# Four-layer graph network on one core: the loads and gathers of layer one's first four chunks wait for an earlier point of the set-up

## What the kernel computes

```python
src = node_irreps[edge_index[0]]
feats = {0: src[:, :M][:, :, None], 1: src[:, M:].reshape(E, M, 3)}
sh = {0: sh0, 1: sh1, 2: sh2}
for idx, (le, ln, lo) in enumerate(COMBOS):
    base = jnp.einsum('ijk,ei,emj->emk', CG[le, ln, lo], sh[le], feats[ln])
    msg[lo] = msg[lo] + jnp.einsum('io,eik->eok', W[idx], base)
agg0 = jax.ops.segment_sum(msg[0].reshape(E, M), tgt, num_segments=N)
agg1 = jax.ops.segment_sum(msg[1].reshape(E, 3 * M), tgt, num_segments=N)
...
x = _layernorm(x + _L0_gnn_ref(x, edge_index, edge_weight1, edge_attr_3, edge_attr_5, L0_gnn_W), axis=-1)
x = _layernorm(x + _L1_gnn_ref(x, edge_attr_2, L1_gnn_weight, edge_index), axis=-1)
x = _layernorm(x + _L2_gnn_ref(...), axis=-1)
x = _layernorm(x + _L3_gnn_ref(...), axis=-1)
```

## Time and profile before

| | us |
|---|---|
| median of 3 runs | 17409.68 (17409.63 to 17410.06) |
| the profiled execution | 17404.72 |
| its span | 17402.7 |
| busy: POOL | 12932.6 (74%) |
| busy: DVE | 12117.7 (70%) |
| busy: PE | 6419.3 (37%) |
| busy: ACT | 3285.1 (19%) |

### The profile page before, as it was taken

How to read it: one execution, slowest core, us unless ns; L and a number is a source line. 1 busy time by engine, 2 the same in 40 slices (tenths; PEclk the granted TensorE clock), 3 DMA queues, 4 the chain that set the end, 5 groups by cost and what they waited for, 6 DMA issues and landing times. The chain is left out here.

```text
span 17402.7 us, 138752 instructions
## 1 busy us (share of the span) xinstructions
PE 6419.3 (37%) x33487; PEld 5142.6 (30%) x33487; DVE 12117.7 (70%) x15588; ACT 3285.1 (19%) x5336; POOL 12932.6 (74%) x13715
## 2 busy tenths in 40 slices
PE   1000000000444454545330000000006999999995
PEld 0000000000333333333320000000005878878774
DVE  5666666674899999999663232223326999999996
ACT  0000000000222222222541101111102223222321
POOL 6777777777677777777757777777777777777776
PEclk9555555555777777777665555555558999999998
DMA  4333333331111111111332222222222222222221
GB/s 103 97 96 97 97 98 97 98 97 47 28 28 28 28 28 28 28 28 25 130 130 59 59 57 59 58 59 58 59 53 45 55 55 53 56 53 56 53 56 36
DMA packets 744244, 1076.69 MB, mean 62 GB/s; under 512 B 375703, under 2 KB 508493, under 8 KB 731294
## 3 DMA queue, kind: packets, MB, share of 16 engines
q0 software_dynamic: 417376, 477.82, 12.5%
q1 hardware_dynamic: 250851, 398.14, 8.2%
q10 hardware_dynamic: 75736, 197.70, 3.1%
HBM read 684.92 MB, written 389.48 MB: 62 GB/s over the span
## 5 line engine op out<-in xcount | busy, mean ns | idle before, releaser
L1937 POOL DMA_INDIRECT s_arena<-d_t,s_arena x3125 | 3086.5, 988 | 971.3 <-issue 943.6
L1898 POOL DMA_INDIRECT d_pay<-s_arena x3125 | 3026.9, 969 | 997.7 <-issue 931.0
L1977 POOL DMA_INDIRECT s_arena<-d_t,s_arena x3125 | 2960.6, 947 | 1032.6 <-issue 952.0
L1955 POOL DMA_INDIRECT s_arena<-d_t,s_arena x3125 | 2948.5, 944 | 981.7 <-issue 952.1
L1649 PE MATMUL psall<-s_arena 128*128 128x500 bf16 x1875 | 835.4, 500 | 4365.4 <-DVE psall L881 3637.1
L992 DVE TENSOR_TENSOR s_arena<-s_arena,psall 128x2400 f32<-128x2400 f32 x125 | 332.0, 2656 | 2712.1 <-DMA s_arena<-d_t,s_arena 2712.1
L1649 PEld LDWEIGHTS psall<-s_arena 128*128 128x128 bf16 x1875 | 222.5, 119 | 4783.3 <-DVE psall L881 3708.7
L1756 PE MATMUL psall<-s_w2r,s_arena 128*128 128x384 f32 x4250 | 1514.0, 491 | 5.9 <-DVE s_arena L1090 5.2
L1838 PE MATMUL psall<-s_tails,s_mfix 128*128 128x32 f32 x6 | 1.9, 412 | 3972.8 <-DVE s_tails L1198 3972.8
L1756 PEld LDWEIGHTS psall<-s_w2r,s_arena 128*128 128x128 f32 x4250 | 1271.0, 317 | 64.3 <-DVE s_arena L1090 6.1
L1099 DVE TENSOR_REDUCE s_arena<-s_arena 128x64 f32<-128x1024 f32 x875 | 1248.1, 1438 | 0.0
(11 more groups left out here) (304 smaller groups left out, 17923.9 us busy)
## 6 DMA issues: line engine op xcount, KB each, us to landing
s_arena<-d_t,s_arena POOLq DMA_INDIRECT x9375, 2.5
d_scan<-s_arena ACTq DMA_DIRECT2D x313, 400.0 KB, 2.6
s_arena<-d_ew SPq DMA_DIRECT2D x126, 800.0 KB
s_arena<-d_pay SPq DMA_DIRECT2D x33, 1650.0 KB, 6.8
d_inj<-s_agg SPq DMA_DIRECT2D x125, 400.0 KB, 3.9
s_arena<-d_inj SPq DMA_DIRECT2D x125, 400.0 KB, 3.4
d_pay<-s_arena POOLq DMA_INDIRECT x3125, 2.2
d_fold<-s_arena ACTq DMA_DIRECT2D x33, 1250.0 KB, 4.9
```

Source lines behind the costliest of these rows:

```text
L1898: e.indirect_dma_start(pay_d, bass.IndirectOffsetOnAxis(ap=S1.adr[s4][:, t:t + 1], axis=0), S1.pay[s4][:, 33 * t:33 * t + 33], None).then_ ...
L1937: e.indirect_dma_start(L3.gb[s][:, t], None, T3_d, bass.IndirectOffsetOnAxis(ap=L3.idx[s][:, t:t + 1], axis=0)).then_inc(sem(f"g3_{s}"), 16)
L1955: e.indirect_dma_start(L0.gb[s][:, t * 128:(t + 1) * 128], None, T0_d, bass.IndirectOffsetOnAxis(ap=L0.idx[s][:, t:t + 1], axis=0)).then_i ...
L1977: e.indirect_dma_start(L2.gb[k][:, t * 96:(t + 1) * 96], None, T2_d, bass.IndirectOffsetOnAxis(ap=L2.idx[k][:, t:t + 1], axis=0)).then_inc ...
```

## The change

`room0(c)` takes the place of `v0(c - 4, "g")` in the two waits of layer one. For chunks 0 to 3 it is `mk["split"]`, from chunk 4 on what it was. So that the four chunks have numbers known in Python, chunks 0 to 4 are written out on SP and POOL, and the loop has 30 rounds. The same transfers are started in the same order, and the other three engines' code is the same.

```diff
--- before.py
+++ after.py
@@ -838,6 +838,10 @@
         def v0(c, name):
 
             return c * PER0 + (mk["base0"] + AT0[name])
+
+        def room0(c):
+
+            return mk["split"] if isinstance(c, int) and c < 4 else v0(c - 4, "g")
 
         def vector_scan0(e, c, s2):
 
@@ -1947,9 +1951,9 @@
 
         def gpsimd_chunk0(e, c, i, k):
             s = k % 4
-            e.wait_ge(sem(f"ix_{s}"), nth4(0 if i is None else i, k) * 16)
+            e.wait_ge(sem(f"ix_{s}"), nth4(i, k) * 16)
             held(e)
-            e.wait_ge(dv.h, v0(c - 4, "g"))
+            e.wait_ge(dv.h, room0(c))
             held(e)
             for t in range(T):
                 e.indirect_dma_start(
@@ -1959,11 +1963,11 @@
         def gpsimd_edges0(e):
             for s in range(4):
                 e.wait_ge(sem(f"t0_st{s}"), 16 * (7 if s == 0 else 6))
-            assert v0(-4, "g") >= mk["split"]
-            gpsimd_chunk0(e, 0, None, 0)
-            with e.Fori(0, 31) as i:
+            for c in range(5):
+                gpsimd_chunk0(e, c, 0, c)
+            with e.Fori(0, 30) as i:
                 for k in range(1, 5):
-                    gpsimd_chunk0(e, i * 4 + k, i, k)
+                    gpsimd_chunk0(e, i * 4 + (k + 4), i + 1, k)
 
         def gpsimd_edges2(e):
             barrier(e, "gpsimd")
@@ -2126,12 +2130,12 @@
 
         def sync_chunk0(e, c, i, k):
             s = k % 4
-            e.wait_ge(dv.h, v0(c - 4, "g"))
+            e.wait_ge(dv.h, room0(c))
             e.sem_inc(idle2, 1)
             e.dma_start(L0.idx[s].bitcast(I32), src_v[:, bass.ds(c * T, T)]).then_inc(sem(f"ix_{s}"), 16)
             for o, w_, a_ in ((0, 1, ew1), (1, 3, ea3), (4, 5, ea5)):
                 e.dma_start(L0.at[s][:, o * T:(o + w_) * T], a_.rearrange("(p t) d -> p (t d)", p=P)[:, bass.ds(c * (T * w_), T * w_)]).then_inc(sem(f"at0_{s}"), 16)
-            if i is None:
+            if k == 0:
                 lo_, n = 0, 14
             else:
                 lo_, n = i * (106 * 33) + (14 + 27 * (k - 1) - (k == 4)) * 33, 26 + (k < 3)
@@ -2139,10 +2143,11 @@
             e.dma_start(inj_d[0:E, :].rearrange("(p t) f -> p (t f)", p=P)[:, bass.ds(c * 800, 800)], agg[:, 924:1724]).then_inc(sem("fill_z"), 16)
 
         def sync_edges0(e):
-            sync_chunk0(e, 0, None, 0)
-            with e.Fori(0, 31) as i:
+            for c in range(5):
+                sync_chunk0(e, c, 0, c)
+            with e.Fori(0, 30) as i:
                 for k in range(1, 5):
-                    sync_chunk0(e, i * 4 + k, i, k)
+                    sync_chunk0(e, i * 4 + (k + 4), i + 1, k)
             e.wait_ge(sem("fill_p"), 125 * 16)
             e.wait_ge(sem("fill_z"), 125 * 16)
```

## The result

| | median us | runs | lowest to highest |
|---|---|---|---|
| kernel before | 17410.3 | 22 | 17408.1 to 17416.7, and one of 29563.9 |
| changed kernel | 17381.4 | 22 | 17377.1 to 17391.8 |

The ratio is 0.9983, with a 95% interval of 0.9977 to 0.9990, which is 17 to 40 us; the single run of 29563.9 is left out of it. The medians differ by 28.9 us. The sum in the prediction was 28.3, and it had 0.94 on a change within 0.2%. That the two lie 0.6 us apart is closer than this interval can show.

What follows compares the result with a forecast made beforehand. POOL's unbroken row of gather starts was taken to bound layer one; 29.3 - 0.5 - 0.5 = 28.3 us off the median 17409.7 gives 17381.4, range 17375 to 17393.

Steps and rivals of the forecast that it cites:

- The bound: Layer one is one unbroken row of POOL gather starts, 1.2483 us apart; starting it earlier gains as much, 29.31 us.
- Late issue and crowded engines: POOL's 29.6 us idle before layer one: SP issues its load late, at 182.39, and it lands slowly beside edge_weight, 18.4 us.
- First cost: SP's 3.6 MB for four chunks now run beside the set-up's last 12 block gathers: 0 to 4.0 us, 0.5 taken.
- Second cost: First gathers now run beside VectorE's last set-up steps, which may hold their starts: 0 to 8.2 us, 0.5 taken.
- Third cost: First gathers of layer one land late beside ACT's edge_weight, but 57 us of cover before chunk 4 make it 0.
- Rival 1: In layer one POOL's queue holds only 9 gathers beside edge_weight, losing 10 us: 17391, at the extreme 17423; chance 0.08.
- Rival 2: Chunk 0's source numbers still come late, or another POOL wait ends last; nothing gained, 17409.7; chance 0.03.
- Rival 3: Layer one's starts lose their even pace as VectorE's steps hold some: 137 us added, 17519; chance 0.03.
- The marks: Times the changed kernel's profile should show, from SP's first load at about 156.5 to POOL's last gather at about 4073.

Runs made afterwards that it cites:

- POOL's old wait: Changed kernel with the old wait put back on POOL's gathers alone, SP's loads still early; 17422.9 us against 17440.3 of the kernel before, ratio 0.9989.
- pieces in the kernel before: Kernel before with ACT's edge_weight issued in 125 pieces, one with each chunk, instead of one transfer; 17426.4 us against 17440.3, ratio 0.9991.
- The four-fold `edge_weight`: Changed kernel with three more transfers like edge_weight's, into a tensor nobody reads; 17460.5 us, ratio 1.0011 against the kernel before.

## Why the prediction was right, point by point

- **The bound.** An unbroken row of POOL starts, and a gain of what its first start moves. Right on the chips where POOL is the bound: the first gather moved 29.3, 17.6 and 15.4 us (changed, POOL's old wait, pieces in the kernel before; the first against the split) and the time 28.9, 17.4 and 13.9. The four-fold `edge_weight` gave the same sum with the other sign: -28.9 + 46.6 = +17.7, measured +20.2. The first of these times is from 22 runs of each kernel; the others rest on medians whose intervals are wider than the differences between them. On the slow chips the premise does not hold (VectorE does not wait for the gathers there), and the intervals are too wide to say whether the number does.
- **Late issue and crowded engines.** Both shown, at 12.9 us for the first (what is left when the engines are free, the load's own 2.7 us in it) and 16.7 for the rest. What the prediction didn't say is that POOL's own wait stood right behind SP's load, at 184, and would have kept 12 us of the 29. It took the edit on POOL as done and did not price it.
- **First cost, SP's transfers (0 to 4.0, 0.5 taken).** Measured 0: 14.85 us in three executions, with nothing, 2.8 and 4.2 MB of SP's beside the block gathers, within the cover of 7.5 us each time. In the changed kernel these landed in 3.7 us (median), where I expected 6 to 7 from the table's stores: that row was too dear, and the bound of 4.0, which came from a stretch beside `edge_weight`, does not apply to SP's transfers alone.
- **Second cost, VectorE's set-up (0 to 8.2, 0.5 taken).** Measured 0: the 40 short steps, 8.36 us in all from 176.2 to 190.1, now run beside gathers, and none of these starts takes over 0.95 us. So the bound of 8.2 us, in which every one of these steps of 0.1 to 0.8 us held POOL in full, has no case here. A long step of the split does hold a start (3.23 us instead of 0.94 beside the 3.41 us of line 404). Length alone does not decide it: beside the 8.22 us of line 905, in layer one of the same execution, no start takes over 1.007. What decides it stays open.
- **Third cost, edge_weight (0).** The result was right, but three terms on the way to it were not. The share of POOL's queue was put at 16 packets per us, and a gather at 36 packets, so 0.45 gathers. From 185 to 215 us it is 639 packets, or 21 per us. They carried 1.31 MB, 2 KB each, so a gather is 32 packets (the 0.09 MB of the earlier trace rows was too coarse for this), and 21 per us are 0.67 gathers:

```profile
q10 hardware_dynamic: 9510, 0.95, 88.3%
q0 software_dynamic: 639, 1.31, 40.7%
```

  And the share is not a steady one. POOL's queue from 182 to 194 us, then from 203 to 209:

```profile
q0 software_dynamic: 46, 0.11, 13.8%
```

```profile
q0 software_dynamic: 309, 0.62, 58.6%
```

  For its first 12 us beside `edge_weight` POOL's queue moved next to nothing, 4 packets per us, and then caught up at 50. A window of 3 us, as in the earlier trace rows, does not give the share. So the gathers piled up at the start, 14 at the worst (17.9 us of landing), and not to 17 at the end, and chunk 0 had landed by 219.4 instead of 225. The cover was real and larger than said: SP's load for chunk 4 is issued at 225.4 where POOL would need it at 299. And it was not the shortest one. What would have failed first is ACT: its mask of chunk 0, at 226.4 now, may come until about 313 (an estimate: 359.2 less the 46.6 us of the stop), which holds chunk 5 and not chunk 4.
- **Rival 1, POOL held by its own queue.** Fallen. It put a limit at 9 gathers; up to 14 were under way (17.9 us of landing, one start every 1.25) without one start over 1.007 us, beside one transfer and beside four. How many gathers would fill the queue is not shown: no run shows more than these 14. The extreme of the rival, a queue that gets nothing beside `edge_weight`, was nearly so for the first 12 us.
- **Rival 2.** Fallen: the load is issued 0.2 us behind the split. What it warned of, another wait that hides behind the named one, did exist, and the change removes it too.
- **Rival 3, an uneven pace.** Fallen: 1.2486 against 1.2483 us, 1.0 us over the layer, where 28.3 were needed to undo the gain.
- **The marks.** SP's load at 158.75 (156.5 forecast), the first gather at 174.65 (172 to 177), the last at 4075.2 (4073), the worst landing 17.9 (15 to 25), VectorE's first multiplication at 219.4 (215 to 230), ACT released at 226.1 (220), the barrier 22.9 (23.0). The 2 us of the early marks are the later split of this execution. "Everything behind it earlier by the same 28" holds to the end of layer one (4099.1 against 4125.3, so 26.2) and not beyond it in this one profile, where layer four took back 9.9; over 22 runs it holds (28.9).

## What to carry to other kernels

A profile names the last releaser of an idle time and hides the others: here POOL's own wait would have kept 12 of the 29 us, had only the load been brought forward, and bringing forward only POOL's gives nothing. A wait for buffer space in the first turns of a loop should name the true last reader of that space; the generic count "chunk minus four", carried on below zero, stood for the end of an unrelated set-up. Where the engine that starts earlier is the bound and its row is unbroken, an edit of this kind is worth what it moves that engine's first instruction; on a chip where another engine has become the bound, that sum says nothing by itself.

## What was not expected of the hardware

- Gathers of 128 x 512 bytes beside a transfer in 100-byte pieces get some 21 packets per us in the mean, landing in 14 us in the median and 17.9 at most, and POOL's starts do not notice. The mean hides that the other queue gets next to nothing at first: the gathers 46 packets from 182 to 194 us, and SP none from 182.4 to 191 in the kernel before, where its first load took 18.4 us instead of 1.9. Both stretches lie within the first 14 us of the transfer, issued from 180.9 in the one and 177.5 in the other. Why it is so stays open.
- 4.2 MB of plain transfers in 14 us, 83% of the engines' time, left POOL's gathers at their pace to the hundredth of a us.
- ACT is stuck 45.2 us in one issue of such a transfer, and four of them kept it from its own work until 359.
- The kernel before took 17410 us in the first comparison and 17440, 22643 and 22683 us on the three chips of the experiments. VectorE's busy time in a chunk of the changed kernel is nearly the same where it is slow (22.1 against 21.9 us). On the slow ones the instructions of VectorE and of SP come late (in the chunk shown above, 8 us and more behind the end of line 902 instead of 0.3 at most). The cause stays open.
